# A hybrid block on one core: matrix products in pairs on 64 rows, plain maxima, two-bank operations

## The reference

```
x = x + attn_a(layernorm(x)); x = x + ffn(layernorm(x))
x = x + attn_b(layernorm(x)); x = x + ffn(layernorm(x))
attn: qkv = x @ w_qkv; 32 query heads of 16, 8 key and value heads (4 queries share one),
      rotary on q and k, scores / 4, causal mask, softmax, probs @ v, @ w_o
ffn:  gate = x @ gate_w.T (8 experts, top 2, softmax of the two); x @ base_w.T + base_b
      + 2 * sum over the two experts of weight * (x @ lora_A.T) @ lora_B.T
```

## Time and profile before

| | us |
|---|---|
| median of 3 runs | 756.21 |
| lowest, highest | 751.93, 758.33 |
| span of the profiled execution | 751.8 |
| PE busy | 721.3 |
| DVE busy | 581.3 |
| POOL busy | 531.3 |
| ACT busy | 495.2 |

### The profile page before, as it was taken

How to read it: one execution, slowest core, us unless ns; L and a number is a source line. 1 busy time by engine, 2 the same in 40 slices (tenths; PEclk the granted TensorE clock), 3 DMA queues, 4 the chain that set the end, 5 groups by cost and what they waited for, 6 DMA issues and landing times.

```text
span 751.8 us, 15131 instructions
## 1 busy us (share of the span) xinstructions
PE 721.3 (96%) x4374; PEld 556.0 (74%) x4374; DVE 581.3 (77%) x2756; ACT 495.2 (66%) x1103; POOL 531.3 (71%) x627
## 2 busy tenths in 40 slices
PE   8788989999999999899999999999999999999987
PEld 6756658778877778677787888777788787757655
DVE  5586878797787969678796988879788877879552
ACT  5555667677676767766676876767676776656642
POOL 2375777868586876978678886869788595865541
PEclk9897999999999999999999999999999999999999
DMA  6853434543535356453636535353544625352101
GB/s 209 240 161 72 129 90 114 149 118 98 127 112 135 101 139 167 124 137 97 151 101 177 146 114 118 106 135 102 159 108 125 149 85 117 93 125 85 49 29 57
DMA packets 53516, 91.15 MB, mean 121 GB/s; under 512 B 8948, under 2 KB 22004, under 8 KB 53432
## 3 DMA queue, kind: packets, MB, share of 16 engines
q1 hardware_dynamic: 51128, 89.13, 44.4%
q10 hardware_dynamic: 2304, 1.05, 0.5%
HBM read 24.08 MB, written 10.42 MB: 46 GB/s over the span
## 4 chain that ended last, share of the span: by engine, by line
PE 84%; DVE 4%; POOL 3%; ACT 3%; DMA 2%; issue 2%; SPq 2%; ACTq 0%; POOLq 0%; DVEq 0%
PE T L481 11%; PE SB L465 11%; PE SA L444 7%; PE T L423 6%; PE T L424 6%; PE T L425 6%; PE T L496 4%; PE T L520 4%; PE T L497 4%; PE SA L448 4%; PE T L498 4%; PE T L521 4%; PE T L522 4%; PE T L402 3%; PE T L507 2%
## 5 line engine op out<-in xcount | busy, mean ns | idle before, releaser
L1009 DVE CUSTOM_DVE_ANT_0 SA<-SA,mask 128x128 f32<-128x128 f32 (+1 forms) x1024 | 333.6, 385 | 55.5 <-PE SA L448 27.4
L792 ACT ACTIVATE PT<-SB 128x512 f32<-128x512 f32 x384 | 220.7, 598 | 77.1 <-PE SB L465 57.1
L1179 POOL TENSOR_SCALAR_AFFINE_SELECT PT<-PT 128x512 f32<-128x512 f32 x256 | 164.7, 661 | 66.4 <-ACT PT L792 66.2
L465 PE MATMUL SB<-QK 100*128 100x512 f32 x384 | 156.9, 418 | 6.3 <-ACT PT L792 5.4
L1009 DVE DVE_READ_ACCUMULATOR2_ANT nm<- 128x1 f32 x1024 | 141.0, 138 | 0.0
L423 PE MATMUL T<-XH,WQh 128*128 128x256 f32 x384 | 112.2, 292 | 4.5 <-DVE XL L975 4.5
L424 PE MATMUL T<-XL,WQh 128*128 128x256 f32 x384 | 110.0, 286 | 0.0
L425 PE MATMUL T<-XH,WQl 128*128 128x256 f32 x384 | 109.8, 286 | 0.0
L444 PE MATMUL SA<-QK 96*128 96x512 f32 x256 | 104.3, 425 | 3.3 <-DVE nm L1009 3.0
L465 PEld LDWEIGHTS SB<-QK 100*128 100x128 f32 x384 | 72.7, 192 | 31.4 <-ACT PT L792 11.3
L481 PE MATMUL T<-PT,V 128*32 128x512 f32 x768 | 89.0, 596 | 1.2 <-POOL PT L1179 0.7
(11 more groups left out here) (107 smaller groups left out, 1554.2 us busy)
## 6 DMA issues: line engine op xcount, KB each, us to landing
QK<-Rh SPq DMA_DIRECT2D x64, 256.0 KB, 3.9
QK<-R SPq DMA_DIRECT2D x64, 192.0 KB, 4.0
Qs<-Qf SPq DMA_DIRECT2D x64, 128.0 KB, 2.7
QK<-R SPq DMA_DIRECT2D x64, 128.0 KB, 3.0
ND<-sums SPq DMA_DIRECT2D x62, 128.0 KB, 2.6
mid<-X SPq DMA_DIRECT2D x16, 256.0 KB, 2.0
X<-mid SPq DMA_DIRECT2D x8, 512.0 KB, 4.0
out<-X SPq DMA_DIRECT2D x16, 256.0 KB, 2.0
```

Of the source, the lines that this page charges most:

```text
L465: e.matmul(SB[k % 2][:, :].rearrange("p (j q) -> p j q", j=4), keys(p, 100)[:, u % 2, i // 2, :], queries(p, 100)[:, :, min(i, 1), :], sta ...
L792: e.activation(PT[:, k % RING, :], SB[k % 2][:, :], ACT.Exp, scale=0.25).then_inc(S["ex"], 1)
L1009: ins = e.tensor_tensor_reduce(x, x, mask[:, 256 - n:256], 1.0, LOWEST, ALU.add, ALU.max, nm[:, p % 2, 0, 8 * a + 2 * h + q:8 * a + 2 * h ...
L1179: e.affine_select(out=blk, in_=blk, compare_op=ALU.is_ge, fill=0.0, base=0, pattern=[[0, 4], [1, 128]], channel_multiplier=-1).then_inc(S[ ...
```

## The change

All products contract 64 rows. A helper `step` issues two matmuls, one on partitions 0 to 63 and one on 64 to 127, that write the two banks of a pair; a product of 128 rows is done in steps with `x` = 0 (upper rows to bank 0, lower to bank 1) and `x` = 1 (the other way), so that each bank gets both halves. Transposes are made in the same manner (`cross`), each half of the rows giving 64 columns. In attention the two halves of `QK` are the two key heads of a group, each with 16 x 4 rows: high query with high key, low query with high key, high query with low key, and 16 spare rows. In the spare rows stand the maxima (row 3 and 67) and constants that add the causal mask to the scores of `A`; a second copy of the key blocks carries them, so `QK` grows from 1536 to 1664 columns. `Am` is a plain `tensor_reduce` over two banks, three times per group in place of sixteen instructions. The low half of the maxima (`ml`) is gone and `mr` is one DMA on SP's queue. `ex`, `causal`, `high`, `low`, `oe`, `ox`, `fx`, `fE`, `addbias`, `store` work on 1024 or on both tiles at once. `norm` moves from ACT to DVE, low keys (`kl`) and part of the rotary steps move to DVE. The eight banks are four pairs `PP0` to `PP3` that all calls share. The split path of the last head group (`xq`, `rq`, `mq`, `hq`, `lq`) is gone. All five orders are new; the one of PE has no loop.

```diff
+        PP = [ctx.enter_context(nc.psum_tensor(f"PP{i}", [P, 2, 512], F32)) for i in range(4)]
...
+            def step(t, c, lhs, rhs, x, start, stop, which=(0, 1)):
+                for r in ((0, 1) if not x else (1, 0)):
+                    rows, k = (UP, LO)[r], r ^ x
+                    ins = e.matmul(t[:, k, c], lhs(rows, which[k]), rhs(rows, which[k]), start=start, stop=stop,
+                                   skip_group_check=True)
+                return ins
...
+            def cross(t, c, source):
+                for k, rows in enumerate((UP, LO)):
+                    ins = e.transpose(t[:, k, c:c + 64], source[rows, :], iden[rows, 64 * k:64 * k + 64])
+                return ins
...
+                for wt, xx in ((WQh, XH), (WQh, XL), (WQl, XH)):
+                    for i in range(2):
+                        ins = step(PP[t], slice(256 * i, 256 * i + 256),
+                                   lambda r, b: wt[r, k, (2 * b + i) * P:(2 * b + i + 1) * P],
+                                   lambda r, b: xx[r, xs, c], x, first and wt is WQh and xx is XH and i == 0,
+                                   last and wt is WQl)
...
+            def A(p, i, t, free=None):
...
+                for j in (range(4) if i == 0 else range(2 * i - 2, 2 * i)):
+                    if i == 0:
+                        ins = step(PP[t], slice(128 * j, 128 * j + 128), lambda r, a: queries(g, a, j, 0),
+                                   lambda r, a: keys(g, a, 1), 0, True, True)
+                    else:
+                        ins = step(PP[t], slice(256 * (j % 2), 256 * (j % 2) + 256), lambda r, a: queries(g, a, j, 1),
+                                   lambda r, a: keys(g, a, 2, 2), 0, True, True)
...
+                for a in range(2):
+                    x = QK[64 * a:64 * a + 64, g, 0:1024].rearrange("r (j q t) -> r j q t", j=4, q=2)
+                    ins = e.matmul(PP[t][:, a, :].rearrange("p (j q) -> p j q", j=4), keys(g, a, 4 if i == 2 else 0),
+                                   x[:, :, min(i, 1), :], start=True, stop=True, skip_group_check=True)
...
-                    ins = e.tensor_tensor_reduce(x, x, mask[:, 256 - n:256], 1.0, LOWEST, ALU.add, ALU.max,
...
+                e.tensor_reduce(o, x, AX.X, ALU.max).then_inc(S["m"], 1)
...
+            def mr(p):
+                w.wait_ge(S["mc"], p + 1)
+                e.dma_start(QK[3:P:64, p % 4, 0:1024].bitcast(F32),
+                            mT[:, p % 2, :].bitcast(F32)).then_inc(S[f"md{p % 2}"], 16)
...
+                e.activation(PT[:, k % RING, :].rearrange("p (a x) -> p a x", a=2), PP[t][:, :, :], ACT.Exp,
+                             scale=0.25).then_inc(S["ex"], 1)
...
+            def norm(c, n):
+                f, i, s = int(c == "f"), n % 2, n // 2
+                w.wait_ge(S["np" + c], s + 1)
+                w.wait_ge(S[c + "t"], n)
+                e.tensor_scalar(xn[:, f, :], X[:, 2 * (s % XR) + i, :], mv[:, f, i, 0:1], rs[:, f, i:i + 1], ALU.subtract,
+                                ALU.mult).then_inc(S[c + "xn"], 1)
...
+                e.affine_select(out=blk, in_=blk, compare_op=ALU.is_ge, fill=0.0, base=0,
+                                pattern=[[0, 8], [1, 128]], channel_multiplier=-1).then_inc(S["sel"], 1)
```

A part of the new order of PE and of SP, with each call's pair of banks and what frees it:

```diff
+            B(34, 2, 2, ("ex", 103)); oM(7, 2, 0, 0); oM(7, 3, 0, 0); A(36, 0, 1, ("ex", 104))
+            q01(10, 0, 0, 3, ("fx", 7)); B(35, 0, 2, ("ex", 105)); q01(10, 1, 0, 3); B(35, 1, 0, ("ox", 8))
+            q01(10, 2, 0, 3); q01(10, 3, 0, 3); A(36, 1, 2, ("ex", 106)); q01(10, 0, 1, 3); A(36, 2, 0, ("ex", 107))
...
+            mr(31); xc(14); rd(14); st(34, 1); st(34, 2); st(34, 0); store(5); rr(14); xl(10); st(35, 2); st(35, 1)
+            st(35, 0); mr(32); sw(9, 0); lc(15); xc(15); sw(9, 2); mr(33); rd(15); rr(15); st(36, 2); st(37, 2)
```

More of the change, by code:

```diff
@@ new lines, in q2 @@
+            def q2(s, k, x, t, free=None):
+                weight(w, k if s < NB else 17 + k)
+                w.wait_ge(S["al"], s + 1)
+                released(free)
+                first, last = turn("q2", FIRST if s == 0 else STEPS, s, k, x)
+                xs, c = xi("a", s), slice(k * P, (k + 1) * P)
+                for wt, xx in ((WQh, XH), (WQh, XL), (WQl, XH)):
+                    ins = step(PP[t], slice(0, 256), lambda r, b: wt[r, k, (4 + b) * P:(5 + b) * P],
+                               lambda r, b: xx[r, xs, c], x, first and wt is WQh and xx is XH,
+                               last and wt is WQl)
+                ins.then_inc(S["q2"], 1)
@@ L526, in fW, with oM @@
-            def fW(s, t, free):
+                        p, a = 2 * h + c // 2, c % 2
+                        ins = e.matmul(PP[t][32 * c:32 * c + 32, min(i, 1), :], V[:, s % 2, i // 2, 4 * G + c, :],
+                                       PT[:, (3 * p + i) % RING, 512 * a:512 * a + 512], start=(i < 2), stop=(i != 1),
+                                       skip_group_check=True)
+                ins.then_inc(S["pv"], 1)
+            def oM(s, k, x, t, free=None):
+                weight(w, 4 + k if s < NB else 21 + k)
+                w.wait_ge(S["ol"], 2 * s + 1 + k // 2)
+                released(free)
+                first, last = turn("oM", HALVES, s, k, x)
+                for o, wt in ((OH, WOh), (OH, WOl), (OL, WOh)):
+                    ins = step(PP[t], slice(0, D), lambda r, b: o[r, k, b, :], lambda r, b: wt[r, k, :], x,
+                               first and o is OH and wt is WOh, last and o is OL)
+                ins.then_inc(S["oM"], 1)
@@ new lines, in fA @@
+            def fA(s, k, x, t, free=None):
+                weight(w, 8 + k)
+                w.wait_ge(S["fl"], s + 1)
+                released(free)
+                first, last = turn("fA", STEPS, s, k, x)
+                c = slice(k * P, (k + 1) * P)
+                step(PP[t], slice(0, 272), lambda r, b: XH[r, 2 + b, c], lambda r, b: WG[r, k, :], x,
+                     first, False)
+                ins = step(PP[t], slice(136, 272), lambda r, b: XL[r, 2 + b, c], lambda r, b: WG[r, k, 0:136], x,
+                           False, last)
+                ins.then_inc(S["fA"], 1)
@@ new lines, in fB @@
+            def fB(s, k, x, t, free=None):
+                weight(w, 12 + k)
+                w.wait_ge(S["fl"], s + 1)
+                released(free)
+                first, last = turn("fB", STEPS, s, k, x)
+                c = slice(k * P, (k + 1) * P)
+                for xx, wt in ((XH, WBh), (XH, WBl), (XL, WBh)):
+                    ins = step(PP[t], slice(0, D), lambda r, b: xx[r, 2 + b, c], lambda r, b: wt[r, k, :], x,
+                               first and xx is XH and wt is WBh, False)
+                ins.then_inc(S["fB"], 1)
```

1696 lines of the change are left out of this document (819 added, 877 removed).

## The result

The changed kernel takes 823.23 us (median of 4 runs, 820.4 to 828.44) against 756.61 in runs of the kernel before beside it (751.93 to 758.33). The ratio is 1.0906, 95% interval 1.0854 to 1.0957: slower by 67 us, where I had forecast 58 less. The profiled execution's own time is 821.8 us.

What follows compares the result with a forecast made beforehand. The prediction took TensorE (PE), 96% busy, as the bound: 751.8 us less 74 saved in attention plus 16 of bank-pair allowance gave 694 in the profile, 698 as measured median. Own range 682 to 740; wider range with rivals 655 to 800.

Steps and rivals of the forecast that it cites:

- PE's model: PE matmul distances per slot: paired 64-row matmuls overlap, 0.119 us at 256 columns, 0.233 at 512; new slot 38.3 us.
- (b): PE weight loads: pairs share the way for weights, a pair costs 0.238 us; +248 us, 946 in all; chance 0.06.
- (c): PE's instruction supply: with a 45 ns floor a short pair costs 0.18 us; +152 us, 850 in all; chance 0.07.
- (d): Faster than forecast: 128-column pairs on PE at 0.06 us and no added waits, 30 us less, 668; chance 0.12.
- The prices of the large pieces: DVE maxima 1.24 us each, ACT exponentials 1.02 each, POOL's 8 causal selects 10.6 us a slot at most.
- the small pieces given to DVE: Per slot on DVE: four normalisations 2.8 us, low keys 1.0, one rotary sum 0.4, one low half of queries 0.7.
- `mr` on SP: Maxima's DMA moved from ACT's queue to SP's: costed at nothing, since M2 comes several steps before the B needing it.
- They cost nothing as long as PE is the longest: Work on DVE, POOL and ACT lies beside PE's 38.3 us slot, at 86%, 84% and 68% busy, adding no time.
- allowance of 1.0 us a slot: Added for handing over the four shared PSUM bank pairs: 16 us in all; could be 0 or several us a slot.
- rival (a): Shared bank pairs turn into PE waits in A and B; 0.35 us a step gives 817; chance 0.15 of 740 to 820.
- my 74 us: PE's saving in attention: B 2.80 and A 1.82 us, together 4.6 us a slot, over 16 slots.
- The start and the end: Reordered weight loads and wider constant fill at the start, no split path at the end: 0 +- 6 us, taken as 0.

Runs made afterwards that it cites:

- the one with three chains shortened: Changed kernel with mu not waiting for the reciprocals' DMA round trip, maxima over one bank only, six batches in ring X instead of five: 767.15 us, ratio 1.0155.
- no trip and one bank: Changed kernel with mu not waiting for the reciprocals' DMA round trip and maxima taken over one bank of the pair only: 780.90 us, ratio 1.0375.

## Why the prediction was wrong

**PE's model held.** Pairs overlap (0.23, 0.12, 0.10 us); the slot's 39.8 us busy at a mean clock of 0.93 are some 37 at full clock, and the sum has 38.3 less 1.0 of old waits. Rivals (b), shared way for weights, and (c), PE's instruction supply, are refuted: pairs of 256 columns would have stood 0.24 or 0.16 to 0.18 apart. (d) named the 128-column pairs at 0.06; they are at 0.10. What the Trainium skill says (TensorEngine Tiling (Array Packing), Key Properties), that different tiles load and multiply in parallel, this trace agrees with. Its 81 ns for a load with a 128-column matmul (TensorE: Matmul & The Clock Gate, Back-to-back issue gap) would be 0.162 a pair; the pairs at 0.10 and 0.12 don't show it.

**The prices of the large pieces held** within 10%: maxima, exponentials, selects. Those of the small pieces given to DVE did not, though DVE's sum came out near: low keys 2.1 us a slot for 1.0, the rotary sum 0.88 for 0.4, the low half of the queries 1.14 for 0.7, a normalisation 0.78 for 0.69. I had priced them as if DVE worked alone. Of the normalisations that the trace shows singly, the 25 with nothing on POOL at the time took 0.53 to 0.55 us; all 24 that took over 0.6, up to 2.1, lay beside an operation of POOL. `mr` on SP cost nothing that can be told, as said.

**The step that failed** is "They cost nothing as long as PE is the longest", with its allowance of 1.0 us a slot. PE is not the longest: it stands some 6.5 us a slot and works part of the rest at the lower clock, 46.1 us for the 38.3 and 1.0 of the sum. I read a slot as a ring of steps through the queues of PE, ACT, DVE, POOL and SP: PV, copy, four DMAs, reciprocal, `mu`, `oh`, `ol`, product with w_o, residual, statistics, `power`, norm, transposes, mixture, store, load. Its length is set by the steps' durations and by what stands in front of each in a queue, not by PE's sum. The busy shares say nothing of it. In the changed kernel each piece is one of 1.0 to 1.3 us, where it was 0.3 to 0.7 per tile, and a step starts only when both tiles or both banks are there; that this is why the ring got longer is argued from the piece lengths and from one run, the one with maxima over one bank (28 us for 90 us of DVE work). That the steps of the other queues set the slot, and not PE's sum, is shown: relief of PE gave 3 to 4 of 30 us in the changed kernel and 2 of 30 in the one with three chains shortened, while shortening three steps with none of PE's work taken away gave 57. How much the shared pairs of banks (rival (a)) add to it no run tells apart.

**The deeper fault is in the sum itself.** I took 4.6 us a slot off PE and counted all of it. The kernel before gives back only 8 to 10 of 30 us. By that rate, an extrapolation from one place in the slot to another, my 74 us were worth some 20 to 25 before anything was added. The rate is no constant: two thirds in the steady slots, nothing in the early ones. (43.00 of 43.00) had looked like proof that PE was the bound. It wasn't: with 1.87 us of its work gone the same view still says 41.76 of 42.00, since modelled ends cover short gaps. The distances, 41.9 of 42.9, were the better reading.

**Rival (a)** had the right side and nearly the size, 3.8 us a slot over the old one for 3.2, 817 for 823. Its mechanism is a part of it: the waits on maxima and exponentials in PE's list are about 34 of 136 us. What it lacked is the round trip, the norm and the SP queue, so that 817 came so near is in part luck. Its 0.15 was too low for something whose threshold I had worked out as 0.19 us per step.

**The start and the end**, "0 +- 6", were +14.6 and +6. PE waits 13 us at the start in one piece, until 50.97, for the copy of the second batch's keys and values. On ACT that copy stands behind the high halves of the first batch's queries, for which ACT itself waits 13.3 us for DVE's rotary sum, and behind high halves of weights, and then it waits 1.4 us for DVE's low keys.

**Left open.** 767 less 698 is 69 us. 13 of it are the start; eight of the slots there still take 43.5 us for the 39.3 forecast (the PV groups of its PE timeline at 288.88 and 636.64), which is another 33, and which of the remaining waits is worth what wasn't told apart. No order that I tried beats the kernel before; the best with right results is 803.

## What to carry to other kernels

Before counting work taken from a full engine as time, leave some of it out in the kernel as it is and see what comes back: here 30 us gave 8 to 10, and that one run would have warned that most of the forecast gain wasn't there. Where the order of five queues is packed by hand, merging operations into larger ones can lengthen the hops from engine to engine even if the busy time falls; count the hops that a result makes between two products, with what stands in front of each, and not only the sums. The moves within such queues gave 20 us once, nothing that can be told three times, and cost 9, 13, 16 and 17 us the other four times: every one has to be run. And a piece given to DVE can cost twice its price while POOL works: read its price where both work.

## What the runs showed of the hardware

Matmuls on rows 0 to 63 and 64 to 127 that write two banks run fully together, down to 256 columns (0.12 us a pair); at 128 columns the pair costs 0.10, above half of that. PE's granted clock is 0.50 in the 5 us behind a wait of 5.2 us (no trip and one bank), and behind one of 4.1 us a PV group goes from 2.78 to 5.12 us. A reduction over 1024 PSUM elements a row in two banks takes 1.215 us. An exponential over as many takes 1.026, where two of 512 took 1.20: the merge saves 0.17 us. Operations of DVE on SBUF get slower while POOL works: a normalisation of 512 elements 0.53 to 0.55 us without POOL, and 0.53 to 2.1 beside it; the low keys of a slot 0.88 to 2.8 us. Operations of DVE that read PSUM do not: the low halves of X kept 1.16 to 1.22 us beside POOL. The store of both tiles in one DMA lands after 5.4 us, in the profile after (page part 6: KB, us to landing); that of one tile was at 2.0 in the profile before.

```profile
mid<-X SPq DMA_DIRECT2D x8, 512.0 KB, 5.4
```

```profile
mid<-X SPq DMA_DIRECT2D x16, 256.0 KB, 2.0
```
